# Routed rows brought back by transfers that add into the shared rows, in a two-layer attention and mixture-of-experts kernel

## The chip, the cores and the metric

The program runs on one core of a Trainium2 chip (trn2), in float32 throughout. The metric is the device time of one execution in microseconds (us), median over runs; lower is better. The core has five engines with instruction queues of their own: PE (matrix products), DVE (vector work), ACT (activations), POOL (general work) and SP (which only issues transfers here). Sixteen DMA engines move data for all of them.

## The reference

Four blocks run one after the other on `x` of shape (2, 512, 256), that is 1024 tokens of 256 values. Each block adds its normalised output to `x`:

```
x = x + layernorm(L0_attn(layernorm(x)))
x = x + layernorm(L0_ffn(layernorm(x)))
x = x + layernorm(L1_attn(layernorm(x)))
x = x + layernorm(L1_ffn(layernorm(x)))
```

The two `ffn` blocks are mixtures of experts, and the change is in what follows them:

```
logits = x @ router_w                      # 8 experts
expert_idx = argmax(logits); score = sigmoid(max(logits))
xs = x * score
out[i] = (silu(xs[i] @ gate_w[e]) * (xs[i] @ up_w[e])) @ down_w[e]     for e = expert_idx[i]
shared = (silu(x @ shared_gate_w) * (x @ shared_up_w)) @ shared_down_w
return out + shared
```

So each token has a routed row (from its one expert) and a shared row, and their sum goes into a layer norm over its 256 values.

## The kernel before, in words

Tokens lie in 8 tiles of 128 rows, one row per partition: tiles 0 to 3 are the first half, 4 to 7 the second. `x`, `y` and `y_shared` are SBUF tensors of 8 such tiles (128 partitions by 8 by 256 float32, 1 KB for each row). The program is written engine by engine, and semaphores tie the engines together; within one engine instructions run in the order of the text.

**A mixture of experts** (`sp_moe`, `pool_moe`, `dve_moe`, `act_moe`, `pe_moe`, once per layer `l`). The router picks an expert for each token. POOL scatters the tokens' rows to a DRAM tensor sorted by expert (line 618). SP fetches them back in 15 tiles of sorted rows, `xg` (line 437); each row carries its score and the number of its token. There are 23 units of work: 8 shared tiles and 15 routed tiles. Units 0 to 5 are the shared tiles 0 to 5, then come the 15 routed tiles, and last the shared tiles 6 and 7. For each unit PE computes the products with gate and up (`gate_up`), ACT and DVE make `h`, PE transposes it and computes the product with down. DVE copies the result from PSUM (line 876, `take_down`): a shared tile into `y_shared`, a routed tile into one of four buffers `yr`. For each routed tile POOL issues an indirect transfer (line 624) which stores the 128 rows of `yr` to a DRAM tensor `routed_y` at the place of their tokens; four semaphores `yr_stored` count their landings.

**What brings the rows back.** SP waits until all 15 stores have landed (lines 445 and 446), then issues four plain transfers (lines 448 and 449, issued through the helper on line 344, so the profile shows line 344). Each brings two tiles, 256 KB, from `routed_y` into `y`, with a semaphore of its own, `gathered[l][0..3]`. In layer 0 SP then goes on with `shared_loads(sp, 1)`, which waits for the last gate/up and down products of layer 0, and with the loads of layer 1's weights: three of shared weights and 24 of experts' weights, each 256 KB, and the padding of the sorted tensor.

**What DVE does with them.** `moe_y` (line 950) waits for the pair's transfer and adds `y_shared` to `y` for a tile (line 953). `y_tiles` (line 678) does that for two tiles, and then takes the statistics of each (`tile_stats`, line 666). `close_stats` (line 668) aggregates four tiles and makes variance and mean (lines 673 to 676), from which POOL computes `rstd` by a power (line 531) and `shift` (line 533). `sum_x` (line 688) adds `y * rstd` to `x` (line 695). `stats_x` takes the statistics of the new `x`. The order on DVE after layer 0 is written out in lines 768 to 776: tiles 0 and 1, tiles 2 and 3, close of half 0, tiles 4 and 5, then `close_x(1, 0)` (sum, statistics of `x`, close), tiles 6 and 7, close of half 1, `close_x(1, 1)`, and only then attention of layer 1. After layer 1 (lines 783 to 789) it is tiles 0 to 3, close, tiles 4 to 7, close, then all eight sums; ACT adds the shift (line 988) and SP stores each tile (line 390).

**What POOL does between.** In layer 0 POOL runs `order_heads` (line 550) after its 15 stores: nine copies that reorder the weights of layer 1's attention (lines 558 and 560). Then come the powers (line 531) of the next halves.

**PE between the layers.** Lines 1118 to 1121: PE waits for the first add on DVE, runs 25 filler products (`keep_warm`), waits for the variance of `x`'s first half, runs 5 more, then transposes the normalised `x` (line 1111) and computes the attention's projections (line 1564).

The semaphore `y_ready` counts DVE's writes of `y`; 8 for each of the four blocks before the change.

Of the kernel before, what the change touches and what calls it, by code (L numbers as in the profile page):

```python
# [24 lines left out]
ALU = mybir.AluOpType  # L25
# [3 lines left out]
P = 128  # L29
B, S, D = 2, 512, 256  # L30
NT = B * S // P
TB = S // P
# [16 lines left out]
NR = NT + E - 1  # L49
NSF = 6  # L50
NXG = 8
NU = NT + NR
REGION = B * S
SORTED = E * REGION + (NR - NT) * P
# [25 lines left out]
def build(nc, a, out):  # L80
    ctx = ExitStack()
    with ctx:
# [20 lines left out]
        x = at("x", [P, NT, D], F32, here)  # L103
# [239 lines left out]
        def load(eng, dst, src, s):  # L343
            return eng.dma_start(dst, src).then_inc(s, 16)
# [83 lines left out]
        def sp_moe(sp, l):  # L428
            sp.wait_ge(expert_ready[l], 2)
            first_rows = [sp.value_load(row[0:1, r:r + 1], min_val=0, max_val=SORTED - P) for r in range(4)]  # L430
            sp.wait_ge(scattered[l], 16 * NT)

            def fetch(r):
                if r >= NXG:
                    sp.wait_ge(yr_stored[l][(r - NXG) % 4], 16 * ((r - NXG) // 4 + 1))
                at_row = first_rows[r] if r < 4 else sp.value_load(row[0:1, r:r + 1], min_val=0, max_val=SORTED - P)
                load(sp, xg[r % NXG][:], sorted_x[l][bass.ds(at_row, P), :], xg_loaded[l][r % NXG])

            for r in range(NR):
                fetch(r)  # L440
            if l == 0:
                load(sp, wqkv_in[:], a["L1_attn_Wqkv"].rearrange("(c p) n -> p c n", p=P), l1_loaded)
                load(sp, bqkv_in[:], a["L1_attn_bqkv"].partition_broadcast(P), l1_loaded)
                load(sp, wo1[:], a["L1_attn_Wo"].rearrange("(c p) n -> p c n", p=P), l1_loaded)
            for i in range(4):
                sp.wait_ge(yr_stored[l][i], 16 * len([r for r in range(NR) if r % 4 == i]))
            rows = routed_y[l][SORTED:, :].rearrange("(t p) d -> p t d", p=P)
            for t in range(0, NT, 2):
                load(sp, y[:, t:t + 2, :], rows[:, t:t + 2, :], gathered[l][t // 2])
            if l == 0:  # L450
                shared_loads(sp, 1)
                for e in range(E):
                    expert_gate_up(sp, 1, e)
                    expert_down(sp, 1, e)
                pad_rows(sp, 1)
# [146 lines left out]
        def pool_moe(pool, l):  # L602
            g = nc.gpsimd

            g.iota(xn_id[:, :, D:D + 1].bitcast(U32), pattern=[[P, NT], [0, 1]], base=SORTED,
                   channel_multiplier=1).then_inc(numbered, 1)
            pool.wait_ge(numbered, l + 1)
            pool.wait_ge(zeroed, 32 * (l + 1))
            for half in range(2):
                sl = slice(half * TB, (half + 1) * TB)  # L610
                pool.wait_ge(xn_ready[half], (2 * l + 2) * TB)
                pool.wait_ge(score_ready[l], half + 1)
                g.tensor_scalar(xn_id[:, sl, D + 1:D + 2], half_score[:, sl].unsqueeze(2), 0.5, 0.5, ALU.mult,
                                ALU.add).then_inc(score_put[l], 1)
                pool.wait_ge(score_put[l], half + 1)
                pool.wait_ge(slot_ready[l], half + 1)
                for t in range(half * TB, (half + 1) * TB):
                    g.indirect_dma_start(sorted_x[l][:, :], bass.IndirectOffsetOnAxis(ap=slot[:, t:t + 1], axis=0),
                                         xn_id[:, t, :], None).then_inc(scattered[l], 16)
            if l == 0:  # L620
                pool_l1(pool)
            for r in range(NR):
                pool.wait_ge(yr_ready[l], NSF + r + 1)
                g.indirect_dma_start(routed_y[l][:, :], bass.IndirectOffsetOnAxis(  # L624
                    ap=xg[r % NXG][:, D:D + 1].bitcast(U32), axis=0), yr[r % 4][:], None).then_inc(yr_stored[l][r % 4], 16)
            if l == 0:
                order_heads(pool)


        CASTS = 10  # L630

        def vector_program(dve):
# [31 lines left out]
            def tile_stats(src, t):  # L664

                mark(v.bn_stats(stat[:, t, :], src[:, t, :]))  # L666
# [11 lines left out]
            def y_tiles(p, tiles, make_y):  # L678

                for t in tiles:  # L680
                    make_y(t)
                for t in tiles:
                    dve.wait_ge(y_ready, p * NT + t + 1)
                    tile_stats(y, t)

            sums_from = [0, 0]

            def sum_x(p, half):

                sums_from[half] = count[0]  # L690
                dve.wait_ge(rstd_ready[1], 2 * (2 * p + half) + 1)
                if p:
                    dve.wait_ge(x_summed, (p - 1) * NT + (half + 1) * TB)
                for t in range(half * TB, (half + 1) * TB):
                    ins = v.scalar_tensor_tensor(x[:, t, :], y[:, t, :], rstd[1][:, t:t + 1], x[:, t, :],
                                                 ALU.mult, ALU.add)
                    if p == BLOCKS - 1:
                        ins.then_inc(last_summed, 1)
                    else:
                        mark(ins)  # L700
# [64 lines left out]
                y_tiles(0, pair, l0_y)  # L765
            close_stats(1, 1)
            close_x(0, 1)
            moe_y = dve_moe(dve, link, 0, normalise_x)
            y_tiles(1, range(0, 2), moe_y)
            y_tiles(1, range(2, 4), moe_y)  # L770
            close_stats(1, 0)
            y_tiles(1, range(4, 6), moe_y)
            close_x(1, 0)
            y_tiles(1, range(6, 8), moe_y)
            close_stats(1, 1)
            close_x(1, 1)
            l1_y = dve_l1(dve, link, mark, settle, y_tiles, close_stats, sum_x)
# [2 lines left out]
                y_tiles(2, (t,), l1_y)  # L780
            close_stats(1, 1)
            close_x(2, 1)
            moe_y = dve_moe(dve, link, 1, normalise_x)
            for half in range(2):
                for t in range(half * TB, (half + 1) * TB, 2):
                    y_tiles(3, (t, t + 1), moe_y)
                close_stats(1, half)
            for half in range(2):
                sum_x(3, half)
# [65 lines left out]
        def dve_moe(dve, link, l, normalise_x):  # L855
# [85 lines left out]
            for i in range(3, NU + 1):  # L941
# [3 lines left out]
                    take_down(u)  # L945
                if NT <= i < 2 * NT:
                    complete(i - NT)
            dve.wait_ge(yr_ready[l], NU)

            def moe_y(t):  # L950
                if t % 2 == 0:
                    dve.wait_ge(gathered[l][t // 2], 16)
                v.tensor_tensor(y[:, t, :], y[:, t, :], y_shared[:, t, :], ALU.add).then_inc(y_ready, 1)

            return moe_y


        def scalar_program(act):
# [138 lines left out]
        def tensor_program(pe):  # L1097
            mm = nc.tensor.matmul

            def turn_x(p, parts):  # L1100

                if p == 0:
                    pe.wait_ge(consts, 4)
                for i in parts:
                    bank_no = TURN_X[p][i]
                    if bank_no in TURN_X[p][:i]:
                        pe.wait_ge(xT_ready, 4 * p + TURN_X[p].index(bank_no) + 1)
                    for t in (2 * i, 2 * i + 1):
                        pe.wait_ge(xn_ready[t // TB], TB * p + t % TB + 1)
                        for c in range(KC):  # L1110
                            last = nc.tensor.transpose(ps[bank_no][:, c * 256 + t % 2 * P:c * 256 + (t % 2 + 1) * P],
                                                       xn[:, t, c * P:(c + 1) * P], ident[:])
                    last.then_inc(xT_made, 1)

            pe_l0(pe, turn_x)
            keep_warm(10, 0)
            pe_moe(pe, 0, turn_x)
            pe.wait_ge(y_ready, NT + 1)
            keep_warm(25, 2)
            pe.wait_ge(var_ready[0], 10)  # L1120
            keep_warm(5, 2)
            pe_l1(pe, turn_x)
            pe_moe(pe, 1, turn_x)
# [97 lines left out]
        def pe_moe(pe, l, turn_x):  # L1221
# [48 lines left out]
            def gate_up(u):  # L1270
# [3 lines left out]
                if r is None:  # L1274
                    if u == 0:
                        pe.wait_ge(shared_w[l], 48)
                    if l and u < 2:
                        pe.wait_ge(y_ready, 2 * NT + TB + 1 + u)
                    t = shared_tile(u)
                    pe.wait_ge(xT_ready, 4 * p + t // 2 + 1)  # L1280
                    for c in range(KC):
# [272 lines left out]
        def pe_l1(pe, turn_x):  # L1554
# [99 lines left out]
            def project(t):  # L1654

                if t < TB:
                    pe.wait_ge(att0_copied, t + 1)
                    if t:
                        pe.wait_ge(y_ready, 2 * NT + t)
                else:  # L1660
                    pe.wait_ge(att1_copied, t - TB + 1)
                    if t == TB:
                        pe.wait_ge(y_ready, 2 * NT + TB)
                for c in range(KC):
                    last = mm(PROJ_BANK[t][:, 0:D], xT[:, c, t * P:(t + 1) * P], wo1[:, c],
                              start=(c == 0), stop=(c == KC - 1))
                last.then_inc(proj_made, 1)
# [160 lines left out]
```

## Time and profile before

| | us |
|---|---|
| median of 3 runs | 675.0 (671.65, 675.63, 675.0) |
| the profiled execution, its own time | 669.68 |
| its span, first to last instruction | 667.8 |
| around the span | 1.88 |
| PE busy | 617.4 (92%) |
| DVE busy | 404.4 (61%) |
| ACT busy | 325.1 (49%) |
| POOL busy | 213.2 (32%) |

Every duration below is from the profiled execution, whose times are counted from the start of the span. It is one execution, and it was 5.3 us shorter than the median of the runs.

### The profile page before, as it was taken

To read this page: it belongs to the slowest core of one execution; us is meant where nothing else is said; L and a number is where in the kernel's file an instruction comes from. 1 tells how busy PE (TensorE), PEld (TensorE's weight loads), DVE (VectorE), ACT (ScalarE), POOL (GpSimd) and SP (SyncE) were. 2 spreads that over 40 slices of the span, in tenths; PEclk is the share of its full clock that TensorE was granted. 3 is DMA by queue.
4 is the path that set the end of the run, shared out by engine and by line. 5 is a ranking of instruction groups with operands and counts; after the bars stand their busy time and mean duration, and the time that the engine had idled before them with its cause. 6 is when DMAs were issued, how large, how long until landed. Compare 5 with 4: busy or idle time off the path is not lost.

```text
span 667.8 us, 11795 instructions
## 1 busy us (share of the span) xinstructions
PE 617.4 (92%) x4298; PEld 408.0 (61%) x4298; DVE 404.4 (61%) x929; ACT 325.1 (49%) x645; POOL 213.2 (32%) x312
## 2 busy tenths in 40 slices
PE   3999999999999988799978999999999999989990
PEld 2887887887888785366665544444444445546660
DVE  4526705632760587533366999989998954743336
ACT  4523423433332224133215589898988875523322
POOL 5870561282073154513333031201010100331331
PEclk9999999999999999899989999999999999999996
DMA  6000200300199992222379994000000000031213
GB/s 220 33 1 33 96 1 20 107 1 1 38 283 299 78 314 77 78 58 81 105 237 346 303 180 3 1 1 2 2 1 2 1 2 1 9 104 55 81 56 126
DMA packets 69000, 57.40 MB, mean 86 GB/s; under 512 B 21520, under 2 KB 64400, under 8 KB 68944
## 3 DMA queue, kind: packets, MB, share of 16 engines
q1 hardware_dynamic: 66736, 50.60, 31.2%
q0 software_dynamic: 2208, 6.05, 2.5%
q8 instruction: 36, 0.59, 0.4%
q14 instruction: 20, 0.16, 0.1%
HBM read 30.78 MB, written 25.85 MB: 85 GB/s over the span
## 4 chain that ended last, share of the span: by engine, by line
PE 73%; DVE 16%; DMA 3%; ACT 3%; issue 2%; POOL 1%; SPq 1%; ACTq 0%; POOLq 0%; DVEq 0%
PE psum L303 9%; PE psum L305 8%; PE psum L304 8%; PE psum L1289 8%; PE psum L1634 8%; DVE mx L1744 7%; PE psum L1606 5%; PE psum L1318 5%; PE psum L1594 5%; PE psum L1619 3%; PE psum L1213 2%; DVE stat L666 2%; PE psum L1564 2%; PE psum L1282 2%; PE psum L1199 1%
## 5 line engine op out<-in xcount | busy, mean ns | idle before, releaser
L1744 DVE TENSOR_REDUCE mx<-psum 128x1 f32<-128x512 f32 x256 | 157.6, 681 | 17.6 <-PE psum L1606 17.5
L1505 ACT ACTIVATE pr<-psum 128x512 f32<-128x512 f32 x256 | 138.0, 598 | 27.9 <-PE psum L1619 26.1
L1634 PE MATMUL psum<-pr,vals 128*32 128x256 f32 x1024 | 77.6, 389 | 0.0
L1619 PE MATMUL psum<-qT,kT 32*128 32x512 f32 x256 | 76.6, 494 | 0.7 <-ACT pr L1505 0.7
L1606 PE MATMUL psum<-kT,qT 32*128 32x512 f32 x256 | 67.7, 488 | 1.7 <-ACT qT L1472 0.7
L1289 PE MATMUL psum<-w_gu,xgT 128*128 x120 | 56.4, 592 | 0.0
L624 POOL DMA_INDIRECT routed_y<-yr,xg x30 | 28.7, 958 | 86.1 <-DVE yr L876 85.5
L1606 PEld LDWEIGHTS psum<-kT,qT 32*128 32x128 f32 x256 | 26.3, 181 | 43.9 <-issue 21.4
L1546 POOL CAST mp<-mx 128x16 bf16<-128x16 f32 x16 | 3.1, 196 | 150.5 <-DVE mx L1744 150.5
L867 DVE SCALAR_TENSOR_TENSOR h<-psum,xg,sg 128x256 f32<-128x256 f32 x30 | 14.5, 484 | 49.8 <-ACT sg L1046 49.8
L1046 ACT ACTIVATE sg<-psum,xg 128x256 f32<-128x256 f32 x30 | 14.2, 474 | 60.4 <-PE psum L1289 60.4
L1013 ACT ACTIVATE q<-psum 128x512 f32<-128x512 f32 x32 | 19.1, 597 | 48.9 <-PE psum L305 48.9
L1634 PEld LDWEIGHTS psum<-pr,vals 128*32 128x32 f32 x1024 | 22.2, 108 | 29.8 <-issue 17.8
L585 POOL TENSOR_TENSOR ksum_t<-k_hi 128x1024 f32<-128x1024 f32 x8 | 19.2, 2401 | 64.6 <-DVE k_lo L814 64.4
L1619 PEld LDWEIGHTS psum<-qT,kT 32*128 32x128 f32 x256 | 34.4, 181 | 8.9 <-ACT pr L1505 4.0
L1019 ACT ACTIVATE q_hi<-q 128x512 fp32r<-128x512 f32 x32 | 20.2, 633 | 40.1 <-DVE q L845 40.1
L303 PE MATMUL psum<-kvo_hi,q_hi 128*128 128x256 f32 x128 | 38.0, 297 | 1.9 <-POOL q_lo L599 1.9
L531 POOL TENSOR_TENSOR rstd<-var,mhalf 128x4 f32<-128x4 f32 x16 | 16.5, 1028 | 64.8 <-DVE nmean L676 64.8
L304 PE MATMUL psum<-kvo_lo,q_hi 128*128 128x256 f32 x128 | 36.1, 282 | 0.0
L305 PE MATMUL psum<-kvo_hi,q_lo 128*128 128x256 f32 x128 | 36.1, 282 | 0.0
L819 DVE TENSOR_TENSOR nk<-psum,same_head 128x8 f32<-128x8 f32 x16 | 1.9, 161 | 53.0 <-PE psum L1191 53.0
L814 DVE SCALAR_TENSOR_TENSOR k_lo<-psum,k_hi 128x512 fp32r<-128x512 f32 x32 | 22.0, 689 | 18.1 <-ACT k_hi L1007 18.0
(214 smaller groups left out, 1406.6 us busy)
## 6 DMA issues: line engine op xcount, KB each, us to landing
sorted_x<-zeros SPq DMA_DIRECT2D x2, 9088.0 KB, 39.2
w_gu<-in_L_ffn_gate_w SPq DMA_DIRECT2D x16, 256.0 KB, 6.2
w_gu<-in_L_ffn_up_w SPq DMA_DIRECT2D x16, 256.0 KB, 6.3
w_d<-in_L_ffn_down_w SPq DMA_DIRECT2D x16, 256.0 KB, 6.6
xg<-sorted_x SPq DMA_DIRECT2D x30, 129.0 KB, 2.2
wk_f<-in_L_attn_Wk SPq DMA_DIRECT2D x4, 512.0 KB, 5.2
wq_f<-in_L_attn_Wq SPq DMA_DIRECT2D x4, 512.0 KB, 6.0
wv_f<-in_L_attn_Wv SPq DMA_DIRECT2D x4, 512.0 KB, 3.7
```

Source lines behind the costliest of these rows:

```text
L303: nc.tensor.matmul(o, lhs[0], rhs[0], start=start, stop=False, **kw)
L304: nc.tensor.matmul(o, lhs[0], rhs[1], start=False, stop=False, **kw)
L305: return nc.tensor.matmul(o, lhs[1], rhs[0], start=False, stop=stop, **kw)
L624: g.indirect_dma_start(routed_y[l][:, :], bass.IndirectOffsetOnAxis(ap=xg[r % NXG][:, D:D + 1].bitcast(U32), axis=0), yr[r % 4][:], None). ...
L1289: last = mm(ps[2 + u % 2][:], xgT[r % 2][:, c], w_gu[:, bass.ds(experts[r], 1), c, :], start=(c == 0), stop=(c == KC - 1))
L1318: last = mm(ps[6 + u % 2][:, 0:D], hT[u % 2][:, c], w, start=(c == 0), stop=(c == FC - 1))
L1505: nc.scalar.activation(pr[d % 3][:, j], s2_bank(d, j), ACT.Exp, scale=SCALE).then_inc(exp_ready, 1)
L1594: last = nc.tensor.transpose(into[:, t * P:(t + 1) * P], src, ident[:])
L1606: mm(s1_bank(c, j), qT1[n % 2][rows, t * P:(t + 1) * P], kT[n // GH][rows, :], start=True, stop=True).then_inc(s1_made, 1)
L1619: mm(s2_bank(d, j), kT[n // GH][rows, kc * P:(kc + 1) * P], qT2[n % 2][rows, :], start=True, stop=True).then_inc(s2_made, 1)
L1634: last = mm(ps[AV_BANK][j * VW:(j + 1) * VW, cols], vals[:, n // NKV * TB + kc, n % NKV // GH * GH + j, :], pr[d % 3][:, j, cols], start=( ...
L1744: v.tensor_reduce(mx[n % 2][:, t, j:j + 1], s1_bank(c, j), AX.X, ALU.max, negate=True).then_inc(max_read, 1)
```

## The change

SP's wait for the stores and its four transfers are taken out. POOL does both, after `order_heads` in layer 0: its transfers read `routed_y` and add into `y_shared` instead of writing `y`. Before the transfer of tiles 6 and 7 POOL also waits until DVE has written all shared tiles. DVE's adds (line 953), eight in each layer, are gone: DVE waits for the pair and takes the statistics of `y_shared`, and `sum_x` reads `y_shared` after the mixtures. `y_ready` now counts the attention blocks alone, so that its wait values shrink. PE's filler products wait for the first pair's transfer in place of the first add.

```diff
@@ sp_moe
-            for i in range(4):
-                sp.wait_ge(yr_stored[l][i], 16 * len([r for r in range(NR) if r % 4 == i]))
-            rows = routed_y[l][SORTED:, :].rearrange("(t p) d -> p t d", p=P)
-            for t in range(0, NT, 2):
-                load(sp, y[:, t:t + 2, :], rows[:, t:t + 2, :], gathered[l][t // 2])
             if l == 0:
                 shared_loads(sp, 1)
@@ pool_moe
             if l == 0:
                 order_heads(pool)
+            for i in range(4):
+                pool.wait_ge(yr_stored[l][i], 16 * len([r for r in range(NR) if r % 4 == i]))
+            rows = routed_y[l][SORTED:, :].rearrange("(t p) d -> p t d", p=P)
+            for t in range(0, NT, 2):
+                if t == NSF:
+                    pool.wait_ge(yr_ready[l], NU)
+                g.dma_start(y_shared[:, t:t + 2, :], rows[:, t:t + 2, :], accum_op=ALU.add).then_inc(gathered[l][t // 2], 16)
@@ vector_program
                 for t in tiles:
-                    dve.wait_ge(y_ready, p * NT + t + 1)
+                    dve.wait_ge(y_ready, p // 2 * NT + t + 1)
                     tile_stats(y, t)
+
+            def moe_tiles(l, tiles):
+
+                for t in tiles:
+                    dve.wait_ge(gathered[l][t // 2], 16)
+                    tile_stats(y_shared, t)
...
-                    ins = v.scalar_tensor_tensor(x[:, t, :], y[:, t, :], rstd[1][:, t:t + 1], x[:, t, :],
+                    src = y_shared if p % 2 else y
+                    ins = v.scalar_tensor_tensor(x[:, t, :], src[:, t, :], rstd[1][:, t:t + 1], x[:, t, :],
                                                  ALU.mult, ALU.add)
...
-            moe_y = dve_moe(dve, link, 0, normalise_x)
-            y_tiles(1, range(0, 2), moe_y)
-            y_tiles(1, range(2, 4), moe_y)
+            dve_moe(dve, link, 0, normalise_x)
+            moe_tiles(0, range(0, 4))
             close_stats(1, 0)
-            y_tiles(1, range(4, 6), moe_y)
+            moe_tiles(0, range(4, 6))
             close_x(1, 0)
-            y_tiles(1, range(6, 8), moe_y)
+            moe_tiles(0, range(6, 8))
             close_stats(1, 1)
             close_x(1, 1)
...
-            moe_y = dve_moe(dve, link, 1, normalise_x)
+            dve_moe(dve, link, 1, normalise_x)
             for half in range(2):
-                for t in range(half * TB, (half + 1) * TB, 2):
-                    y_tiles(3, (t, t + 1), moe_y)
+                moe_tiles(1, range(half * TB, (half + 1) * TB))
                 close_stats(1, half)
@@ dve_moe
-            dve.wait_ge(yr_ready[l], NU)
-
-            def moe_y(t):
-                if t % 2 == 0:
-                    dve.wait_ge(gathered[l][t // 2], 16)
-                v.tensor_tensor(y[:, t, :], y[:, t, :], y_shared[:, t, :], ALU.add).then_inc(y_ready, 1)
-
-            return moe_y
@@ tensor_program
-            pe.wait_ge(y_ready, NT + 1)
+            pe.wait_ge(gathered[0][0], 16)
             keep_warm(25, 2)
@@ pe_moe, pe_l1: the counts of y_ready
-                        pe.wait_ge(y_ready, 2 * NT + TB + 1 + u)
+                        pe.wait_ge(y_ready, NT + TB + 1 + u)
...
-                        pe.wait_ge(y_ready, 2 * NT + t)
+                        pe.wait_ge(y_ready, NT + t)
...
-                        pe.wait_ge(y_ready, 2 * NT + TB)
+                        pe.wait_ge(y_ready, NT + TB)
```

## Rows read from the trace of the kernel before

**Rows 1.** The page: span, and the last chain's shares by engine.
```profile
span 667.8 us, 11795 instructions
...
PE 73%; DVE 16%; DMA 3%; ACT 3%; issue 2%; POOL 1%; SPq 1%; ACTq 0%; POOLq 0%; DVEq 0%
```

**Rows 2.** The chain that ended last, 330 to 356 us (start, us, what).
```profile
334.32 2.40 DMA routed_y<-yr,xg
...
336.87 3.19 DMA y<-routed_y
...
344.96 1.66 DVE x L695 x4
...
348.76 1.06 POOL rstd L531
...
352.73 3.49 PE psum L1564 x10
```

**Rows 3.** The same chain from 645 us to the end.
```profile
649.05 2.42 DMA routed_y<-yr,xg
...
651.61 2.86 DMA y<-routed_y
...
661.33 0.40 DVE x L695
```

**Rows 4.** Timeline of DVE after layer 0 (start, us, instructions).
```profile
338.14 0.42 DVE L876 COPY y_shared<-psum 128x256 f32<-128x256 f32 x1 [1.68 <-PE psum L1318]
...
342.21 0.74 DVE L666 BATCH_NORM_STATS2 stat<-y 128x6 f32<-128x256 f32 x2
...
344.22 0.74 DVE L666 BATCH_NORM_STATS2 stat<-y 128x6 f32<-128x256 f32 x2
344.91 1.71 DVE L695 SCALAR_TENSOR_TENSOR x<-y,rstd,x 128x256 f32<-128x256 f32 x4
```

**Rows 5.** Timeline of DVE after layer 1.
```profile
659.90 0.74 DVE L666 BATCH_NORM_STATS2 stat<-y 128x6 f32<-128x256 f32 x2
...
661.23 3.25 DVE L695 SCALAR_TENSOR_TENSOR x<-y,rstd,x 128x256 f32<-128x256 f32 x8
```

**Rows 6.** DVE's groups by line, 652 to 667 us (busy us, mean ns).
```profile
L953 DVE TENSOR_TENSOR y<-y,y_shared 128x256 f32<-128x256 f32 x8 | 3.0, 412 | 1.3 <-DMA y<-routed_y 1.3
```

**Rows 7.** Timeline of POOL at the end of layer 0.
```profile
333.06 0.96 POOL L624 DMA_INDIRECT routed_y<-yr,xg  x1 [1.84 <-DVE yr L876]
334.32 0.96 POOL L624 DMA_INDIRECT routed_y<-yr,xg  x1 [0.30 <-issue]
...
337.18 0.28 POOL L560 COPY bqkv<-bqkv_in 128x128 f32<-128x128 f32 x1
```

**Rows 8.** Timeline of SP's transfers around the end of layer 0.
```profile
316.43 0.44 SPq L344 DMA_DIRECT2D wqkv_in<-in_L_attn_Wqkv  x1
...
336.87 2.89 SPq L344 DMA_DIRECT2D y<-routed_y  x4
339.85 0.41 SPq L344 DMA_DIRECT2D shared_gu<-in_L_ffn_shared_gate_w  x1
```

**Rows 9.** Line 624, the store issued at 318.6 us: duration (ns), time to landing.
```profile
L624 POOL DMA_INDIRECT routed_y<-yr,xg x1: 959/959/959, 318.6 to 318.6; - x1
...
DMA to landing us min/median/max: 3.8/3.8/3.8
```

**Rows 10.** Line 624, the store issued at 324.7 us.
```profile
L624 POOL DMA_INDIRECT routed_y<-yr,xg x1: 961/961/961, 324.7 to 324.7; - x1
...
DMA to landing us min/median/max: 2.4/2.4/2.4
```

**Rows 11.** Windows: length, PE, PEld, DVE, ACT, POOL busy, PE clock, DMA share, GB/s.
```profile
343.00:345.00 2.00, 2.00 (x11) 2.00 (x10) 1.97 (x11) 0.00 (x0) 1.13 (x2) 0.50 0.89 263
345.00:350.00 5.00, 4.43 (x36) 4.10 (x35) 4.90 (x19) 0.00 (x0) 1.31 (x3) 0.97 1.05 345
...
653.00:654.00 1.00, 0.00 (x0) 0.00 (x0) 0.30 (x1) 0.00 (x0) 0.00 (x0) 1.00 0.96 285
```

## The prediction, made before the changed kernel was run

> **What bounds the kernel now.** I read the page first. The span is 667.8 us, and its last chain is 73% PE and 16% DVE, with 3% for transfers [rows 1]. A change that takes work from DVE and gives POOL transfers is therefore decided in the few places where the chain leaves PE. The chain in order of time shows two: after each mixture it runs through the last store of routed rows, the transfer back, and DVE's statistics [rows 2, 3]. I then read the timelines of DVE, POOL and SP around those two places.
>
> *After layer 0.* The last store is issued at 334.32 and lands 2.40 later, at 336.7. SP issues its four transfers at 336.87, and the first lands 3.19 later, at 340.06 [rows 2]. DVE adds and takes statistics; those of tiles 2 and 3 begin at 342.21, those of tiles 4 and 5 at 344.22, and the sums of half 0 at 344.91 [rows 4]. The sums lead to POOL's power at 348.76 and to the projections of attention at 352.73 [rows 2]. Everything later in layer 1 follows, so I take a shift of these sums one for one.
>
> *After layer 1.* The transfer back is issued at 651.61 and lands 2.86 later [rows 3]. The statistics of the last two tiles begin at 659.90 and the eight sums at 661.23 [rows 5]. Output follows the sums, so the end also shifts one for one with them.
>
> **The change part by part.**
>
> *The adds.* Sixteen adds at 412 ns go, 6.6 us of DVE's time; the eight of layer 1 took 3.0 with what lies between [rows 6]. The four transfers in layer 1 are over soon after the first has landed, so all eight adds lie on the path there: about 2.6 us, the 3.0 us less what overlaps neighbours. In layer 0 four lie on it, those of tiles 0 to 3, some 1.3 us. Those of tiles 4 and 5 are hidden behind POOL's power, and those of tiles 6 and 7 come when half 0 is already with ACT. But once the adds are gone DVE is not late any more: the transfers are, and the question is when each lands.
>
> *When POOL can issue.* SP could issue at 336.87 [rows 8]. POOL ends the last of nine copies at 337.18 + 0.28 = 337.46 [rows 7], and between two of its transfers stand 0.30 us of issue [rows 7], so the first accumulation is issued at about 337.75, 0.9 later. In layer 1 POOL is idle, and 651.7 against 651.61 is all.
>
> *The pace of the issues.* SP puts out four transfers in 2.89 us, 0.72 each [rows 8]. POOL needs 0.96 for an indirect one of 128 rows plus 0.30 before the next, 1.26 [rows 7]. The new ones have 256 rows each, and the trace holds no POOL transfer of that kind. From below: SP's pace, 0.72, if POOL does a direct transfer as lightly. From above: twice the 0.96 plus 0.30, 2.22. In the middle of 1.26 and 2.22 lies 1.75, which I take, for twice the rows should cost something.
>
> *From issue to landing.* SP's took 2.86 undisturbed [rows 3]. From below the same 2.86. POOL's issue of 0.96 is 0.55 longer than SP's 0.41 [rows 7, 8], which gives 3.4. From above add another 0.96 for twice the rows, and 0.87 for moving the 256 KB a second time at some 300 GB/s (285 in [rows 11]), since an accumulation must read what it adds to: 5.2. I take 4.2.
>
> *What collides.* SP's queue loses a wait. The loads of layer 1's weights followed the transfers back at 339.85 [rows 8]. They will now follow the last down product, which DVE begins to copy at 338.14 [rows 4], so from about 338.2, and all but the first accumulation run beside them. In the trace these loads keep the DMA engines full, at 263 to 345 GB/s [rows 11]. Before, the four transfers were ahead of them in the same queue. The nearest row on the price is a store of POOL issued at 318.6, while 832 KB of loads issued from 316.43 [rows 8] were on their way: it took 3.8 to land against 2.4 undisturbed [rows 9, 10], 1.4 more. From below 0; from above each accumulation gets half of 300 GB/s for twice its bytes, and they land 512 KB / 150 GB/s = 3.5 apart. I take 0.5 on the first and 1.4 on the others. The Trainium skill ("DMA: Bandwidth & Descriptors", section "Queues, rings and completion order") says that each DMA engine serves its queues in turn, packet by packet; by that the upper price holds, and [rows 9, 10] bear it out only in part.
>
> *The sum, layer 0.* Landings: first 337.75 + 4.2 + 0.5 = 342.45; second 337.75 + 1.75 + 4.2 + 1.4 = 345.1; third 346.85; fourth 348.6. DVE starts 0.09 after a landing (340.06 to the first add at 340.15). From the statistics of tiles 2 and 3 to the sums it is 344.91 - 342.21 = 2.70 with POOL's power in it [rows 4]: 345.1 + 0.09 + 2.70 = 347.9. From the statistics of tiles 4 and 5, which stand ahead of the sums on DVE, 0.69: 346.85 + 0.09 + 0.69 = 347.6. The later decides: 347.9 against 344.91, **3.0 later**. The fourth landing is inside what DVE has to do for half 0, and costs nothing.
>
> *The sum, layer 1.* First landing 651.7 + 4.2 = 655.9, fourth 655.9 + 3 x 1.75 = 661.15. From the statistics of tiles 6 and 7 to the sums it is 661.23 - 659.90 = 1.33 [rows 5]: 661.15 + 0.09 + 1.33 = 662.57 against 661.23, **1.3 later**.
>
> *Edits at nothing.* Statistics and sums read another tensor of the same shape. The wait for DVE's shared tiles on POOL is met at 338.14 + 0.42 = 338.56 in layer 0 [rows 4], before POOL comes to its fourth transfer. Behind POOL's four transfers are queued the powers for `rstd`; at 1.75 each POOL is free at 344.75, before the first is wanted at 346.7; at 2.22 it is free at 346.6, just so. PE's filler products start with the first landing and may find PE's clock lower: it was at 0.50 (1.2 GHz) in 343 to 345, after PE's idle time from 338 on, and back at 0.97 in the next five [rows 11]; the projections begin 8 us after that and keep their distance.
>
> Together + 4.3 on 669.68, the profiled execution's own time: 674.0. The median of the runs is 675.0, so the forecast on that footing is **679.3**. A measurement of this kernel tells about 1% (6.75 us) from no change.
>
> A rule that speaks against the change stands in the Trainium skill ("Collectives: The Full Stack", section "The bandwidth ceiling: the fold count and why AG ≠ RS ≠ AR"): an add in the DMA path halves the rate since it needs two reads. By it four transfers of 256 KB at some 300 GB/s come no closer than 1.75 apart even if POOL issues faster, and the faster rival below falls; no row of this kernel shows an accumulation.
>
> **The rivals.**
>
> *Forecast: both places a little later* (net 0 to +6.7). For it: both places wait for a transfer, and POOL's is slower than SP's in every row.
>
> *POOL's transfers are as light as SP's* (the other side). Landing 2.86, pace 0.54 to 0.72, no collision. In layer 1 all four are in by about 656.7 and DVE is the bound: first landing 654.6, and then 661.23 - 654.56 = 6.67 less 2.64 of adds, sums at 658.7, 2.5 earlier. In layer 0 the second lands at 337.75 + 2.86 + 0.6 = 341.2, sums at 344.0, 0.9 earlier. Sum -3.4: 666.3, or 671.6 on the runs' footing. It decides in layer 1 where the fourth landing comes before 659.8 (659.90 less 0.09), that is, with a first landing after 3.4, at a pace under 1.6. With pace 1.26 and landing 3.4: layer 1 -0.9, layer 0 +0.3, so -0.6. Against it: POOL's 0.96 for half the rows.
>
> *The weight loads starve the accumulations.* At the upper prices layer 0 lands at 337.75 + 5.2 + 1.4 = 344.35, then 347.85, then 351.35, and the third decides: sums at 352.1, +7.2. With layer 1 at 5.2 and 2.22 (fourth landing 663.6, sums 665.0, +3.75) that is +10.95: 680.6, or 686. With layer 1 as forecast, +8.5: 683.5. For it: loads without a pause from 338.2, where [rows 9] had only three. Against it: the 1.4 of [rows 9].
>
> *The change does not do what it says* would be adds still on DVE or a wait that holds POOL; nothing in the diff points to it.
>
> **How the numbers follow.** Forecast 62%, lighter than thought 17%, starved 19%, else 2%. Only the outer part of the second kind comes near 1% faster: 2%. Of the starved cases and the forecast's upper edge 20% are beyond 1% slower. Within 1%: 78%. The range reaches from the middle of the lighter case, 672.5, to the starved case without its last microsecond, 685.0.
>
> **What would show it.** In the changed profile: no L953; four POOL transfers after each mixture, 1.3 to 2.2 apart, each 3.4 to 5.2 to landing in layer 1 and longer in layer 0; shared loads on SP from 338.2; DVE idle ahead of the statistics and released by those transfers; sums of half 0 near 347.9, the last eight near 662.6. The forecast is wrong if the fourth transfer of layer 1 lands before 659.8, or if the third of layer 0 lands after 350.

## The result and the profile after

| | us | against the kernel before, 95% interval |
|---|---|---|
| changed kernel, median of 12 | 679.78 (677.98 to 680.45) | ratio 1.0098 (1.0074 to 1.0121) |
| kernel before, median of 12 | 671.42 (669.69 to 677.29) | |
| changed kernel, profiled execution | 679.86, span 678.0 | |

The change makes the kernel about 1% slower, 6.6 us by the ratio (5.0 to 8.1); the two medians lie 8.4 us apart. The two profiled executions lie 10.2 us apart. The one of before was short even for that kernel: PE's mean granted clock was 0.986 in it, while 64 later executions of the same kernel had 0.972 to 0.983. Their time goes with the clock: the 28 at 0.979 or more have a median of 670.9 us, the 36 below it 673.9. All 12 runs of the changed kernel had 0.970 to 0.978. So I compare the two places of the change each from a fixed point, the issue of the last store of routed rows, to the start of DVE's sums.

The page of the changed kernel, the shares by engine of its last chain:

```profile
PE 73%; DVE 14%; DMA 5%; ACT 2%; POOL 2%; issue 2%; SPq 1%; ACTq 0%; POOLq 0%; DVEq 0%
```

DVE lost 2 points against [rows 1], transfers gained 2 and POOL 1 in a longer span: the adds are gone, and more than their time went to the wait for what does them now.

After layer 0, the chain of the changed kernel (start, us, what):

```profile
334.65 0.96 POOL routed_y L619
...
337.77 1.55 POOL y_shared L629 x2
339.32 9.85 DMA y_shared<-routed_y
...
349.95 1.57 DVE x L704 x4
```

Where [rows 2] had 3.19 us of transfer and then DVE's work, 9.85 us of transfer stand now, up to the landing of the third accumulation. POOL's issues there, from its timeline, and then DVE's waits, from its own:

```profile
337.49 0.28 POOL L555 COPY bqkv<-bqkv_in 128x128 f32<-128x128 f32 x1
337.74 5.01 POOL L629 DMA_DIRECT2D y_shared<-routed_y  x4
```

```profile
343.13 0.75 DVE L668 BATCH_NORM_STATS2 stat<-y_shared 128x6 f32<-128x256 f32 x2 [4.23 <-DMA y_shared<-routed_y]
346.94 0.75 DVE L668 BATCH_NORM_STATS2 stat<-y_shared 128x6 f32<-128x256 f32 x2 [3.06 <-DMA y_shared<-routed_y]
...
349.20 0.75 DVE L668 BATCH_NORM_STATS2 stat<-y_shared 128x6 f32<-128x256 f32 x2 [0.81 <-DMA y_shared<-routed_y]
349.87 1.66 DVE L704 SCALAR_TENSOR_TENSOR x<-y_shared,rstd,x 128x256 f32<-128x256 f32 x4
```

Read the brackets: DVE is idle 4.23, 3.06 and 0.81 us ahead of the three pairs of statistics, each time for an accumulation. By DVE's starts they land 5.4, 9.2 and 11.5 us after the first issue. From the last store to the sums it is 349.87 - 334.65 = 15.22 us, against 344.91 - 334.32 = 10.59 before [rows 2, 4]: **4.6 later**.

After layer 1, the same two timelines:

```profile
657.42 0.96 POOL L619 DMA_INDIRECT routed_y<-yr,xg  x1 [0.31 <-issue]
660.47 5.02 POOL L629 DMA_DIRECT2D y_shared<-routed_y  x4 [2.10 <-DMA routed_y<-yr,xg]
```

```profile
664.77 0.75 DVE L668 BATCH_NORM_STATS2 stat<-y_shared 128x6 f32<-128x256 f32 x2 [3.11 <-DMA y_shared<-routed_y]
666.82 0.75 DVE L668 BATCH_NORM_STATS2 stat<-y_shared 128x6 f32<-128x256 f32 x2 [1.29 <-DMA y_shared<-routed_y]
...
668.71 0.75 DVE L668 BATCH_NORM_STATS2 stat<-y_shared 128x6 f32<-128x256 f32 x2 [0.45 <-DMA y_shared<-routed_y]
670.08 0.75 DVE L668 BATCH_NORM_STATS2 stat<-y_shared 128x6 f32<-128x256 f32 x2 [0.61 <-DMA y_shared<-routed_y]
...
671.42 3.25 DVE L704 SCALAR_TENSOR_TENSOR x<-y_shared,rstd,x 128x256 f32<-128x256 f32 x8
```

All four pairs wait, though nothing else uses the DMA engines. 671.42 - 657.42 = 14.00 us against 661.23 - 649.05 = 12.18 before [rows 3, 5]: **1.8 later**. The two places together give 6.4 us, inside the interval of the ratio (5.0 to 8.1) and 2 us short of the difference of the medians. Whether PE's lower clock in the changed kernel's runs makes up the rest, no run settles.

All eight accumulations in one line, durations in ns, and their time from issue to landing in us:

```profile
L629 POOL DMA_DIRECT2D y_shared<-routed_y x8: 1327/1989/2730, 337.7 to 662.8; - x8
...
DMA to landing us min/median/max: 4.3/7.0/11.3
```

### The profile page after: what moved, and what is told of

Its sections match the earlier page's. It is cut to its first block, busy times and chain, and to the rows that moved or that the text cites. A ratio compares the mean times of both kernels' runs of the same rounds, so it can differ in the third digit from the quotient of the medians.

```text
span 678.0 us, 11777 instructions
## 1 busy us (share of the span) xinstructions
PE 622.5 (92%) x4298; PEld 411.2 (61%) x4298; DVE 400.0 (59%) x913; ACT 325.1 (48%) x645; POOL 222.9 (33%) x320
## 4 chain that ended last, share of the span: by engine, by line
PE 73%; DVE 14%; DMA 5%; ACT 2%; POOL 2%; issue 2%; SPq 1%; ACTq 0%; POOLq 0%; DVEq 0%
PE psum L303 9%; PE psum L304 8%; PE psum L305 8%; PE psum L1633 8%; PE psum L1288 8%; DVE mx L1743 7%; PE psum L1605 5%; PE psum L1317 5%; PE psum L1593 5%; PE psum L1618 3%; DMA y_shared<-routed_y 3%; PE psum L1563 2%; PE psum L1212 2%; PE psum L1281 2%; PE psum L1198 1%
## 5 line engine op out<-in xcount | busy, mean ns | idle before, releaser
L1633 PE MATMUL psum<-pr,vals 128*32 128x256 f32 x1024 | 79.1, 396 | 0.0
```

The source lines that it names most:

```text
L1633: last = mm(ps[AV_BANK][j * VW:(j + 1) * VW, cols], vals[:, n // NKV * TB + kc, n % NKV // GH * GH + j, :], pr[d % 3][:, j, cols], start=( ...
```

## The experiments

In this table each run stands with its two places, from the issue of the last store to DVE's sums in its own profile, and with its measured ratio. Each ratio is to the kernel before as it was measured beside that run: its median was 671.4 us beside the changed kernel, 671.9 beside loads_wait, warm, layer0_only and layer1_only, 672.6 beside the two pool_plain and the two mixed kernels, and 673.9 beside heads_after and two_transfers. So medians of different groups are not compared with each other below without the ratios.

| run | layer 0, us | layer 1, us | median, us | ratio to before, 95% interval |
|---|---|---|---|---|
| before | 10.59 | 12.18 | 671.42 to 673.89 | |
| changed kernel | 15.22 | 14.00 | 679.78 | 1.0098 (1.0074 to 1.0121) |
| loads_wait | 12.51 | 14.30 | 676.19 | 1.0076 (1.0056 to 1.0096) |
| warm | 15.20 | 14.16 | 680.68 | 1.0135 (1.0118 to 1.0151) |
| layer0_only | 15.39 | 11.99 | 676.38 | 1.0060 (1.0038 to 1.0082) |
| layer1_only | 10.10 | 14.35 | 673.97 | 1.0029 (1.0012 to 1.0047) |
| pool_plain | 12.19 | 12.84 | 674.72 | 1.0051 (1.0028 to 1.0074) |
| pool_plain_loads_wait | 11.41 | 12.92 | 671.38 | 0.9991 (0.9969 to 1.0013) |
| mixed_l1b | 10.66 | 12.08 | 671.62 | 0.9991 (0.9968 to 1.0014) |
| mixed_l1 | 10.27 | 11.50 | 670.17 | 0.9973 (0.9947 to 0.9998) |
| heads_after | 13.50 | 14.42 | 675.57 | 1.0037 (1.0002 to 1.0072) |
| two_transfers | 16.26 | 14.03 | 679.62 | 1.0091 (1.0061 to 1.0120) |

The places repeat to a few tenths where nothing at them was changed: layer 1 of the changed form in five runs 14.00 to 14.42, layer 0 of the plain form in four runs 10.10 to 10.66. The medians are noisier, so small effects are read at the places.

My theory at this point was that two things cost: the DMA engines are slow when they add, and in layer 0 the weight loads run beside them. The rivals were POOL's issue, PE's clock, and an equal loss at both places.

### The weight loads kept back: loads_wait

```diff
@@ sp_moe, on the changed kernel
             if l == 0:
+                sp.wait_ge(gathered[0][3], 16)
                 shared_loads(sp, 1)
```

> The changed kernel, but SP waits for the fourth accumulation of layer 0 before it loads layer 1's weights. Theory (the weight loads slow the accumulations of layer 0): its four landings come as after layer 1, some 4.3, 6.4, 8.2 and 9.6 us after the first issue instead of 5.4, 9.2, 11.5 and 13.6; the sums of half 0 come 3 us earlier, and the run is 3 us shorter than the changed kernel, up to 6 if PE's clock then stays up. Rival (an accumulation is as slow by itself): landings stay within 0.5 us of those of the changed kernel and the time within 1 us.

DVE's timeline after layer 0:

```profile
342.25 0.75 DVE L669 BATCH_NORM_STATS2 stat<-y_shared 128x6 f32<-128x256 f32 x2 [3.41 <-DMA y_shared<-routed_y]
344.43 0.75 DVE L669 BATCH_NORM_STATS2 stat<-y_shared 128x6 f32<-128x256 f32 x2 [1.42 <-DMA y_shared<-routed_y]
...
346.03 0.75 DVE L669 BATCH_NORM_STATS2 stat<-y_shared 128x6 f32<-128x256 f32 x2 [0.15 <-DMA y_shared<-routed_y]
347.11 1.71 DVE L705 SCALAR_TENSOR_TENSOR x<-y_shared,rstd,x 128x256 f32<-128x256 f32 x4 [0.33 <-POOL rstd L527]
```

The first issue is at 337.71, so the landings come 4.5, 6.6 and 8.2 us after it, as undisturbed in layer 1. The place is 2.7 us shorter (12.51 against 15.22). The collision is shown at the place: three profiles with the loads beside the accumulations have 15.20 to 15.39, the two without them 12.51 and 13.50 (heads_after, below). The whole time says less: the median is 3.6 us lower, but the ratio, 1.0076 against 1.0098, only 1.5, and the two intervals overlap. The remaining 1.9 us over the kernel before are not the loads.

### PE kept busy: warm

```diff
@@ tensor_program, on the changed kernel
+            keep_warm(17, 2)
             pe.wait_ge(gathered[0][0], 16)
-            keep_warm(25, 2)
+            keep_warm(36, 2)
```

> The changed kernel with 17 filler products before PE's wait for the first landing of layer 0 and 36 in place of 25 after it, so that PE has no idle time there. Theory (PE's clock falls in the two idle stretches and costs 0.9 us in the projections of layer 1 and about 2.4 us more in the attention after them): landings unchanged, projections from 357.6 last 5.5 us instead of 6.4, and the run is 1 to 3.3 us shorter. Rival (the clock costs nothing that another engine would not cost): within 0.5 us of the changed kernel.

First the changed kernel, then this one: windows by their times, with length, busy time of PE, PEld, DVE, ACT and POOL, PE's granted clock, share of the DMA engines and GB/s.

```profile
353.60:359.00 5.40, 5.40 (x20) 4.36 (x21) 4.14 (x16) 3.18 (x6) 2.41 (x4) 0.50 1.09 348
...
388.00:390.00 2.00, 1.45 (x12) 0.68 (x5) 2.00 (x5) 1.90 (x4) 0.00 (x0) 1.00 1.12 293
390.00:392.00 2.00, 1.89 (x13) 0.89 (x16) 2.00 (x4) 1.67 (x5) 1.02 (x5) 0.61 1.12 252
392.00:394.00 2.00, 2.00 (x20) 0.55 (x12) 0.96 (x2) 0.57 (x2) 1.99 (x5) 0.50 1.13 259
394.00:396.00 2.00, 2.00 (x16) 0.92 (x12) 1.29 (x2) 1.08 (x2) 0.00 (x0) 0.50 1.15 252
```

```profile
353.00:356.00 3.00, 1.50 (x11) 1.34 (x12) 1.89 (x14) 0.86 (x2) 2.04 (x3) 1.00 1.09 349
...
366.00:380.00 14.00, 13.21 (x59) 9.21 (x58) 8.76 (x15) 7.42 (x16) 0.00 (x0) 0.76 1.11 305
...
394.00:397.00 3.00, 3.00 (x26) 0.94 (x19) 2.46 (x4) 1.57 (x3) 2.15 (x6) 0.50 1.13 270
```

PE's filler products after the first landing, in the changed kernel and then in this one:

```profile
343.15 7.22 PE L1127 MATMUL psum<-ident 128*128 128x128 f32 x50 [4.72 <-DMA y_shared<-routed_y]
```

```profile
343.42 8.30 PE L1128 MATMUL psum<-ident 128*128 128x128 f32 x72 [1.02 <-DMA y_shared<-routed_y]
```

The edit did not take all of PE's idle time away: 1.02 us of 4.72 were left ahead of the first landing, and 2.0 of 3.2 ahead of the variance. But the clock stayed at 2.4 GHz over the hand-over, and the projections took 5.4 us again, where the changed kernel had 6.4. Yet the clock then fell to 0.76 (mean) in 366 to 380 and to 0.50 (1.2 GHz) in 394 to 397, and the run was not shorter: its median is 0.9 us longer, its ratio 1.0135 against 1.0098, with intervals that just overlap. So the theory that the idle time of PE at the hand-over costs this kernel 1 to 3 us fell. The low stretch after 390 us has only some 0.7 us of idle time ahead of it (388 to 391), after 8 us of PE busy throughout, and layer1_only has one too, whose layer 0 is as before. What sets it stays open. It is not plain scatter either: the mean clock of a run differs by kernel (the changed kernel 0.970 to 0.978, mixed_l1 0.983 in eight of twelve runs), so a share of the loss that goes through PE's clock is neither shown nor excluded.

### One layer at a time: layer0_only and layer1_only

```diff
@@ in the layer that is kept as before
 SP:   the waits for yr_stored and the four plain loads into y come back
 POOL: no wait, no transfer
 DVE:  y_shared[t] = y[t] + y_shared[t] ahead of each pair's statistics
```

> Accumulations after layer 0 alone; after layer 1 SP's plain transfers and DVE's adds (which write y_shared). Theory (most of the loss is in layer 0 and follows from it): 6.5 us above the kernel before, 1.8 below the changed one. Rival (the two places cost alike): 4 us above the kernel before.

> Accumulations after layer 1 alone; after layer 0 SP's plain transfers and DVE's adds. Theory: 1.8 us above the kernel before, its fourth landing 9.6 us after the first issue. Rival (the two places cost alike): 4 us above.

layer0_only is 4.0 us slower than before by its ratio (2.6 to 5.5), less than the 6.5 I expected, because I had counted a low stretch of PE's clock as a consequence. The 4.0 is the rival's number, but not for the rival's reason: layer1_only is 1.9 us slower (0.8 to 3.2), as expected, so the two places do not cost alike. Their places say the same, 4.8 and 2.2 longer than before. Together 0.89% against 0.98% of the whole change: the two losses add up.

### POOL's issue without the add: pool_plain and pool_plain_loads_wait

```diff
@@ pool_moe, on the changed kernel; DVE's adds as in the run above
-                g.dma_start(y_shared[:, t:t + 2, :], rows[:, t:t + 2, :], accum_op=ALU.add).then_inc(gathered[l][t // 2], 16)
+                g.dma_start(y[:, t:t + 2, :], rows[:, t:t + 2, :]).then_inc(gathered[l][t // 2], 16)
```

> POOL issues four plain transfers into y after each layer, at the places of the accumulations, and DVE adds as before (into y_shared). Theory (the add in the transfer costs, since it reads twice; POOL's issue costs less): after layer 1 the first lands 3.5 us after the first issue instead of 4.3 and the four 1.0 apart instead of 1.8, the DMA engines move near 300 GB/s instead of 160, and the sums start 1 us later than in the kernel before. Rival (POOL's issue of 256 rows is what is slow): landings as those of the accumulations, and with the adds back the sums start 4 us later than before.

> As pool_plain, and SP's loads of layer 1's weights wait for the fourth transfer of layer 0. Theory (the collision hurts plain transfers too): the sums of half 0 come 1 to 2 us earlier than in pool_plain. Rival (only accumulations are hurt): within 0.5 us of pool_plain.

pool_plain after layer 1, the four transfers in one line (columns as above), and then a window while they move (columns as in the windows of warm):

```profile
L643 POOL DMA_DIRECT2D y<-routed_y x4: 724/746/776, 656.6 to 658.8; - x4
...
DMA to landing us min/median/max: 3.1/3.7/4.1
```

```profile
658.00:660.00 2.00, 0.00 (x0) 0.00 (x0) 0.29 (x1) 0.00 (x0) 1.53 (x3) 0.71 0.90 274
```

The changed kernel, a window while its accumulations move:

```profile
664.00:666.00 2.00, 0.00 (x0) 0.00 (x0) 0.75 (x2) 0.00 (x0) 1.49 (x2) 0.50 1.07 145
```

A plain transfer of 256 rows costs POOL 0.75 us, about SP's 0.72 in [rows 8] (in layer 1 SP starts them 0.5 apart), and lands in 3.1 to 4.1. The accumulations start 0.75 apart too, but the DMA engines, no less busy (1.07 against 0.90), move 145 GB/s instead of 274. That is the cost of the add, shown by itself.

One rival is left, that the accumulations go out in smaller packets. The queue that moves the four transfers after layer 1 (packets, MB, its share of the 16 DMA engines in the window) settles it: SP's plain ones in the kernel before, 651.5 to 658.5 us; POOL's plain ones in pool_plain, 656.5 to 664; the accumulations of the changed kernel, 660 to 671.

```profile
q1 hardware_dynamic: 1088, 1.05, 48.8%
```

```profile
q0 software_dynamic: 320, 1.05, 43.6%
```

```profile
q0 software_dynamic: 1088, 1.05, 65.8%
```

Share times window, the same megabyte takes all 16 engines 3.4, 3.3 and 7.2 us. SP's has as many packets as the accumulations and takes half their time, so it is the add and not the packets. In layer 1 POOL's plain form with DVE's adds is 0.7 us slower than the kernel before; the accumulation adds another 1.2 us although eight DVE adds are gone.

Keeping the loads back shortens layer 0 of the plain form by 0.8 us (12.19 to 11.41), where I expected 1 to 2: plain transfers are hurt as well, but far less than the 2.7 of the accumulations. The ratio of pool_plain_loads_wait came out at 0.9991, equal to the kernel before and better than its places (1.5 us longer) allow. PE's clock goes with that: nine of its ten runs had a mean of 0.982, where 17 of the 34 runs of the kernel before beside it had 0.978 or less. Against the other 17 (median 670.9) its 671.4 is 0.5 longer. Why its clock is higher stays open.

### An add where DVE is busy anyway: mixed_l1b and mixed_l1

```diff
@@ layer 1 only, layer 0 as before; mixed_l1b: pairs 2 and 3, mixed_l1: pair 3
 SP:   plain loads of the other pairs into y, DVE adds them
 POOL: accumulation of tiles 4 to 7 (mixed_l1b) or of tiles 6 and 7 (mixed_l1)
```

> Layer 0 as before (SP's transfers, DVE's adds). After layer 1 SP brings tiles 0 to 3 by plain transfers, which DVE adds, and POOL accumulates tiles 4 to 7 at the same time. Theory (an accumulation is a gain where DVE is busy while it runs): both accumulations land within 7 us of SP's first issue, under DVE's work on half 0, four adds (1.3 us) leave the path, and the run is 1.0 to 1.4 us shorter than the kernel before. Rival (they hold up SP's transfers or land late): 1 us longer or worse.

> As mixed_l1b with the accumulation for tiles 6 and 7 alone. Theory: two adds (0.66 us) leave the path and nothing waits, 0.7 us shorter than the kernel before. Rival: the one accumulation lands late or slows SP's transfers, no gain.

mixed_l1b, DVE's timeline:

```profile
660.47 0.74 DVE L682 BATCH_NORM_STATS2 stat<-y_shared 128x6 f32<-128x256 f32 x2
662.37 0.75 DVE L682 BATCH_NORM_STATS2 stat<-y_shared 128x6 f32<-128x256 f32 x2 [1.16 <-DMA y_shared<-routed_y]
...
663.72 3.25 DVE L728 SCALAR_TENSOR_TENSOR x<-y_shared,rstd,x 128x256 f32<-128x256 f32 x8
```

mixed_l1, POOL's timeline and then DVE's:

```profile
655.15 1.34 POOL L641 DMA_DIRECT2D y_shared<-routed_y  x1 [3.92 <-DVE y_shared L907]
```

```profile
659.78 1.40 DVE L682 BATCH_NORM_STATS2 stat<-y_shared 128x6 f32<-128x256 f32 x4
661.21 0.38 DVE L689 BATCH_NORM_AGGREGATE mv<-stat 128x2 f32<-128x6 f32 x4
```

With two accumulations the first hides and the second lands 1.16 us late, 8.1 us after SP's first issue and not within the 7 I expected, which eats the four adds saved: 12.08 against 12.18. With one, issued at 655.15 and landed 4.5 later, the statistics of four tiles run through without a gap, and the place takes 11.50, 0.7 less, as expected. Its ratio of 0.9973 excludes 1 only narrowly, and it means 1.8 us, more than the place gives; eight of its twelve runs had PE's clock at 0.983. It is the one form here that beats both kernels, by 0.3% and by half a per cent at most, of which the place shows 0.1%.

### The nine copies behind the accumulations: heads_after

```diff
@@ pool_moe, on loads_wait
             if l == 0:
-                order_heads(pool)
             for i in range(4):
...
+            if l == 0:
+                order_heads(pool)
```

> As loads_wait, and POOL issues its accumulations ahead of the nine copies of order_heads. Theory (the copies hold up the first issue by 0.8 us and nothing else): from the issue of the last store of layer 0 to the sums 11.7 us, against 12.5 in loads_wait, and the time 0.8 us below it. Rival (the copies now hold up POOL's power for the sums, or the last landing was never held up by them): 12.5 us or more.

Timeline of POOL:

```profile
334.01 0.96 POOL L620 DMA_INDIRECT routed_y<-yr,xg  x1 [0.30 <-issue]
337.10 5.01 POOL L628 DMA_DIRECT2D y_shared<-routed_y  x4 [2.13 <-DMA routed_y<-yr,xg]
```

The first issue comes 3.09 us after the last store's; with the copies ahead of it (loads_wait) it was 337.71 - 334.60 = 3.11, and in layer 1, where there are none, 3.05. So the copies did not hold it up. What made POOL later than SP (2.55, from [rows 2]) is its own start after the wait: the store has landed 2.4 after its issue, and POOL begins another 0.6 later. My theory fell here, and the second half of the rival's held. With the copies behind, the place even took 1.0 longer than in loads_wait, since the second landing came 7.7 us after the first issue instead of 6.6; whether the copies slow the accumulations was not tried apart. The whole time does not show it: the ratio is 1.0037, below the 1.0076 of loads_wait, with intervals that overlap.

### Two transfers of twice the size: two_transfers

```diff
@@ pool_moe and moe_tiles, on the changed kernel
-            for t in range(0, NT, 2):
-                if t == NSF:
+            for t in range(0, NT, TB):
+                if t == TB:
                     pool.wait_ge(yr_ready[l], NU)
-                g.dma_start(y_shared[:, t:t + 2, :], rows[:, t:t + 2, :], accum_op=ALU.add).then_inc(gathered[l][t // 2], 16)
+                g.dma_start(y_shared[:, t:t + TB, :], rows[:, t:t + TB, :], accum_op=ALU.add).then_inc(gathered[l][t // 2], 16)
...
-                    dve.wait_ge(gathered[l][t // 2], 16)
+                    dve.wait_ge(gathered[l][t // TB * 2], 16)
```

> The changed kernel with two accumulations of four tiles (512 KB) after each layer in place of four of two. Theory (what costs is the DMA engines' rate when they add, 256 KB in about 1.6 us, and not the number of transfers): after layer 1 the first lands about 6 us after its issue, the second about 9.5, and from the last store's issue to the sums it stays within 0.5 us of the changed kernel's 14.0. Rival (a fixed cost of each accumulation): the second lands by 8 us and the sums start 1.5 us sooner.

The two transfers by their line, durations in ns, and their time from issue to landing:

```profile
L629 POOL DMA_DIRECT2D y_shared<-routed_y x2: 1283/1352/1421, 661.1 to 662.6; - x2
...
DMA to landing us min/median/max: 6.3/6.9/7.4
```

The line is of layer 1 alone. The first lands 6.3 after its issue, the second at 662.6 + 7.4 = 670.0, 8.9 after the first issue, and the place takes 14.03 us against 14.00. Half as many transfers, the same bytes, the same time: bytes set the cost, not the number of transfers. (Rows and bytes were halved or kept together in all these runs, so the two are not told apart.) After layer 0 the place is 1.0 longer, 16.26 against 15.22: the sums there wait for tiles 4 and 5, which now come with 6 and 7 and land 12.4 us after the first issue, where they landed after 11.5.

## Why the prediction was right, point by point

It forecast a loss of 4.3 us at two places (679.3 on the footing of a median of 675.0, where the measured one is 679.78). The sign and both places were right; the loss was 6.6 by the ratio and 8.4 by the medians. That the two totals agree within 0.5 us is luck: the median of before came down from 675.0 to 671.4 with more runs. The difference is what tests the working, and by the ratio it was a third short. Both signs of being wrong stayed silent, one narrowly: the fourth landing of layer 1 came at 670.0, which is 661.6 in the times of the kernel before (its last store was issued 8.4 earlier) and so after 659.8, and the third of layer 0 came at 349.2, before 350.

- *From issue to landing*, taken as 4.2: measured 4.3. Right.
- *The pace*, taken as 1.75: in layer 1 the four landings are (9.6 - 4.3) / 3 = 1.77 apart. The size is right and the reason was not. I had it from POOL's issue, between one and two times the 0.96 of [rows 7]; but POOL starts an issue of 256 rows every 0.75 us (pool_plain), and what spaces the landings is the DMA engines' rate when they add. So the 1.75 was luck in its size. The rule that I set beside the sum (the Trainium skill, "Collectives: The Full Stack", section "The bandwidth ceiling: the fold count and why AG ≠ RS ≠ AR") gave the same 1.75 as an estimate. These runs show its halving, 145 GB/s against 274, and 7.2 us of the engines' time against 3.3; that the second read is the reason, as the Trainium skill says there of ReduceScatter, no run shows by itself.
- *When POOL can issue*: I put 0.9 us on the nine copies and the next issue in layer 0 and 0.1 on layer 1. It is 0.5 at both, and has nothing to do with the copies (heads_after). This is most of what layer 1 missed: forecast 1.3, measured 1.8.
- *What collides*: this is the term that was mis-sized. I added 0.5 to the first landing and 1.4 to the others; measured against loads_wait it is 0.9, 2.6 and 3.3 (5.4, 9.2, 11.5 against 4.5, 6.6, 8.2). The 1.4 came from a store of 128 KB beside three loads [rows 9], a transfer that reads once beside loads that end; here each adds, beside loads that do not end. The add matters in it: plain transfers of POOL beside the same loads lost 0.8 where the accumulations lost 2.7. What the unending loads do was not tried apart. The forecast for layer 0 was 3.0, and it was 4.6. The third landing decided, which I had given to the starved case alone. That case put it 13.6 us after the first issue, at 3.5 between landings, and overshot: it came after 11.5, and the landings lie 3.8, 2.3 and 2.1 apart. So layer 0, 4.6 later, lies between the forecast (3.0) and that rival (7.2).
- *The rival on the other side* (POOL as light as SP) was nearly right about the pace of the issue and fell by the add, and by the 0.5 us that POOL starts later than SP. Its condition, a pace under 1.6, was the right one to watch.
- *PE's fillers at nothing*: the projections kept their distance from the sums (7.75 us against 7.82), but they ran at 1.2 GHz in the changed kernel's profile and took 1.0 us more (6.45 against 5.43). With them held at 2.4 GHz the run was no shorter, so I cannot count that time as won or lost.

## What to carry to other kernels

An add folded into a transfer cost the DMA engines about twice the time for the same bytes here (7.2 us against 3.3), so price it against the transfer's own rate and not against the vector instruction that it saves; it paid only where the transfer ended under other work, as for one pair here. When a wait moves from one queue to another, look at what stood behind it in the old queue: SP's loads had followed the transfers back, the change let them start beside the accumulations, and holding them back gave 2.7 us of that place. Compare two traces from a fixed event next to the change, since differences of a few us that go with PE's clock lie between whole spans.

## What the runs showed that I had not expected

- A plain POOL transfer of 256 rows takes POOL 0.72 to 0.79 us, less than an indirect one of 128 rows (0.96). With the add the first takes 1.33 and the fourth 2.73, though they still start 0.75 apart.
- POOL starts a transfer 0.6 us after the landing that it waited for (660.47 after 657.42 + 2.43), SP 0.15 (336.87 after 334.32 + 2.40 in [rows 2]).
- PE's clock falls to 1.2 GHz for some 7 us in attention of layer 1 (after 390 us in the changed kernel's profile) with only 0.7 us of idle time ahead of it; in the profile of the kernel before it does not.
